# Expert halves split earlier in the last batch, and the first plan cut into pieces between the queries

## The reference

```python
def xattn(query, kv):                     # 16 heads of 32
    q, k = feature_map(query @ Wq.T), feature_map(k_part(kv @ Wkv.T))      # x>0: x+1, else exp(x)
    gate = sigmoid(query @ Wg.T + bg)
    z    = 1 / (einsum(q, k.sum(-2)) + 1e-6)
    return (einsum(q, einsum(k, v)) * z * gate) @ Wo.T
def ffn(x):
    w, sel = top_k(x @ Wr, 2);  w = softmax(w)
    return sum_e gate_e * (x @ We[e] + be[e])
x = x + xattn(layernorm(x), ctx)
x = x + ffn(layernorm(x))
```

## Time and profile before

| | us |
|---|---|
| median of 3 runs | 618.32 (618.17 to 620.92) |
| span of the profiled execution, from its first to its last instruction | 623.2 |
| busy in it: PE, DVE, ACT, POOL | 565.5, 343.8, 198.4, 152.9 |

### The profile page before, as it was taken

The page is one execution under the profiler, slowest core; times in us unless marked ns, Lnnn a source line. Parts: engine busy times, 40 slices in busy tenths (PEclk is TensorE's granted clock), DMA queues, the critical chain, the costliest instruction groups (busy, mean ns, idle before and its releaser), DMA issues.

```text
span 623.2 us, 10341 instructions
## 1 busy us (share of the span) xinstructions
PE 565.5 (91%) x2944; PEld 473.5 (76%) x2945; DVE 343.8 (55%) x889; ACT 198.4 (32%) x348; POOL 152.9 (25%) x179
## 2 busy tenths in 40 slices
PE   6999999999999999999999995998679999988750
PEld 4888888888888788888888884887557788766540
DVE  4453276374347456327636449677886544437753
ACT  5555333534442533532443432234001111111100
POOL 3014201014000003200101436029993000054513
PEclk9999999999999999999999998899779999999985
DMA  9713101313100412200131203457557568679956
GB/s 293 265 35 110 60 1 52 121 67 134 36 0 0 168 34 101 101 0 0 57 121 58 101 25 128 153 167 244 192 161 250 168 197 278 212 257 286 402 206 184
DMA packets 39610, 84.50 MB, mean 136 GB/s; under 512 B 4640, under 2 KB 4640, under 8 KB 39584
## 3 DMA queue, kind: packets, MB, share of 16 engines
q1 hardware_dynamic: 23232, 42.75, 21.5%
q0 software_dynamic: 7424, 25.17, 11.9%
q10 hardware_dynamic: 8928, 16.26, 6.9%
HBM read 52.18 MB, written 31.98 MB: 135 GB/s over the span
## 4 chain that ended last, share of the span: by engine, by line
PE 81%; issue 6%; POOL 6%; DVE 3%; DMA 2%; DVEq 1%; ACT 1%; another core or an unknown queue 1%; POOLq 0%; SPq 0%; ACTq 0%
PE pj L1035 22%; PE pj L1037 21%; PE pj L1036 21%; PE tp L1027 5%; PE kvb L1089 5%; POOL R L490 3%; PE pj L1117 3%; PE tp L1097 2%; PE pj L1043 2%; POOL R L488 1%; DMA num<-y,gidx 1%; DVEq L948 1%; POOL wraw L481 1%; ACT L612 1%; DMA wraw<-in_L_xattn_Wkv_dram 1%
## 5 line engine op out<-in xcount | busy, mean ns | idle before, releaser
L1035 PE MATMUL pj<-R 128*128 128x512 f32 x448 | 185.0, 413 | 3.2 <-DVE R L741 3.2
L1037 PE MATMUL pj<-R 128*128 128x512 f32 x448 | 177.4, 396 | 0.0
L1036 PE MATMUL pj<-R 128*128 128x512 f32 x448 | 176.5, 394 | 0.0
L1035 PEld LDWEIGHTS pj<-R 128*128 128x128 f32 x448 | 85.4, 191 | 19.5 <-DVE R L741 4.4
L1037 PEld LDWEIGHTS pj<-R 128*128 128x128 f32 x448 | 85.0, 190 | 19.2
L1036 PEld LDWEIGHTS pj<-R 128*128 128x128 f32 x448 | 85.6, 191 | 15.6
L1035 PE MATMUL pj<-R,aux 128*128 x184 | 78.2, 425 | 20.9 <-issue 17.6
L1037 PE MATMUL pj<-R,aux 128*128 x184 | 73.9, 402 | 0.0
L1036 PE MATMUL pj<-R,aux 128*128 x184 | 73.7, 400 | 0.0
L651 ACT CAST aux<-tp 128x512 fp32r<-128x512 f32 x46 | 26.9, 585 | 114.2 <-PE tp L1097 84.5
L475 POOL TENSOR_TENSOR rstd<-rstd,mhalf 128x1 f32<-128x1 f32 (+1 forms) x20 | 13.2, 662 | 203.0 <-DVE rstd L759 203.0
(11 more groups left out here) (156 smaller groups left out, 743.0 us busy)
## 6 DMA issues: line engine op xcount, KB each, us to landing
khat<-xs SPq DMA_DIRECT2D x46, 256.0 KB
wraw<-in_L_ffn_We_dram POOLq DMA_DIRECT2D x16, 512.0 KB, 3.9
buf<-in_ctx_dram SPq DMA_DIRECT2D x15, 512.0 KB, 3.8
y<-kvbd ACTq DMA_DIRECT2D x23, 256.0 KB
y<-zeros ACTq DMA_DIRECT2D x23, 256.0 KB
wraw<-in_x_dram SPq DMA_DIRECT2D x4, 1024.0 KB, 7.7
x_rows<-gate SPq DMA_DIRECT2D x3, 1024.0 KB, 5.2
out_dram<-wraw ACTq DMA_DIRECT2D x12, 256.0 KB
```

The source lines that it names most:

```text
L1035: nc.tensor.matmul(bank[:, :], s_hi(k), m_hi(k), start=(k == 0), stop=False)
L1036: nc.tensor.matmul(bank[:, :], s_hi(k), m_lo(k), start=False, stop=False)
L1037: last = nc.tensor.matmul(bank[:, :], s_lo(k), m_hi(k), start=False, stop=(k == KT - 1))
```

## The change

The slots of R are dealt out anew: the first four weights stay where they were, the turned tokens take slots 10 and 11 and the output weight 12 and 13. So the slots of experts 3, 4 and 5 hold only the query weight, the gate weight and the turned tokens, none of which is read after the last gate product. GpSimd now splits the first half of expert 3 once the last batch's last q product is done, and lays the other halves of 3, 4 and 5 between and behind the four scales; only experts 6 and 7 wait for the output products. On VectorE the first plan is advanced by one piece behind each of the last batch's qhat instructions, and the four `index` instructions come behind the queries.

```diff
--- before.py
+++ after.py
@@ -66,13 +66,15 @@
         R = sb("R", [P, 2 * E, KT, D], F32R)
         WK, WV, WQ, WG, WO = range(5)
 
+        W_AT = [2, 4, 6, 8, 12]
+
         def w_hi(n):
-            return R[:, 2 + 2 * n, :, :]
+            return R[:, W_AT[n], :, :]
 
         def w_lo(n):
-            return R[:, 3 + 2 * n, :, :]
-
-        xT_hi, xT_lo = R[:, 12, :, :], R[:, 13, :, :]
+            return R[:, W_AT[n] + 1, :, :]
+
+        xT_hi, xT_lo = R[:, 10, :, :], R[:, 11, :, :]
         ctxT_hi = R[:, 14, 0:2, :].rearrange("p s (k c) -> p s k c", k=KT)
         ctxT_lo = R[:, 14, 2:4, :].rearrange("p s (k c) -> p s k c", k=KT)
         agT_hi = R[:, 15, 0:2, :].rearrange("p s (k c) -> p s k c", k=KT)
@@ -516,11 +518,21 @@
             pool.wait_ge(SEMS["v"], nth("v", last, ST - 1))
             for h in range(4):
                 cut_expert(1 + h // 2, h % 2)
-            for t in range(TT):
-                scale(1, t, 1, "_x2", last, t)
+            pool.wait_ge(SEMS["q"], nth("q", last, G - 1))
+            cut_expert(3, 0)
+            scale(1, 0, 1, "_x2", last, 0)
+            cut_expert(3, 1)
+            scale(1, 1, 1, "_x2", last, 1)
+            pool.wait_ge(SEMS["g"], nth("g", last, TT - 1))
+            cut_expert(4, 0)
+            scale(1, 2, 1, "_x2", last, 2)
+            cut_expert(4, 1)
+            scale(1, 3, 1, "_x2", last, 3)
+            cut_expert(5, 0)
+            cut_expert(5, 1)
             pool.wait_ge(SEMS["wo"], nth("wo", last, TT - 1))
             nc.gpsimd.memset(bias[:, :], 0.0).then_inc(zeroed, 1)
-            for e in range(3, E):
+            for e in range(6, E):
                 for h in range(2):
                     cut_expert(e, h)
             for t in range(TT):
@@ -849,7 +861,7 @@
                 link(nc.vector.bn_aggr(mv[:, 1, t, :], stats[:, :]))
                 centre(1, t, 1, "mean_x2")
 
-            def queries(b):
+            def queries(b, planning=()):
                 for step, kind, i in QUERIES:
                     if step == "T" and kind == "c":
                         if b is LAST:
@@ -862,6 +874,7 @@
                         dve.wait_ge(SEMS["expq"], nth("expq", b, i))
                         nc.vector.scalar_tensor_tensor(qhat[:, i, :], expq[:, i % 2, :], 1.0, qhat[:, i, :],
                                                        ALU.min, ALU.add).then_inc(SEMS["qhat"], 1)
+                        next(planning, None) if b is LAST else None
                     elif step == "G":
                         if i == 0:
                             dve.wait_ge(x2_stored, b * 16 + 16)
@@ -937,11 +950,9 @@
                 keys(b + 1, b)
                 assert n_step[0] == start + per, (n_step, start, per)
             n_step[:] = [start + per * (B - 1), 0, 0]
-            for _ in plan(0, vones.rearrange("p s g c -> p (s g c)")):
-                pass
+            queries(B - 1, plan(0, vones.rearrange("p s g c -> p (s g c)")))
             for c in range(4):
                 index(c, c)
-            queries(B - 1)
 
             def copy_y(m, slot, n):
```

## The result

The changed kernel takes 618.08 us (median of 20 runs, 616.25 to 619.89) against 619.85 us for the kernel before in 20 runs (617.49 to 622.73): a ratio of 0.9967, 95% interval 0.9956 to 0.9978. By the ratio that is 2.0 us less, where 0.6 us more was forecast. It is small, but the interval leaves no doubt of its sign. The forecast time, 618.9 us, lies only 0.8 us from 618.08, but that is luck: it was built on 618.32 us for the kernel before, which takes 619.85 us over these 20 runs.

The account below looks back on a forecast made before the run. TensorE bounds the kernel, idling where GpSimd's splits hold VectorE, at the last batch's queries and in START. Terms 5.0 + 1.0 + 1.5 - 6.9 = +0.6 us on the 618.32 median gave 618.9 us, range 611.5 to 625.

Parts of the forecast that it names:

- Term 1: At the last batch's queries, held plan pieces on VectorE delay qhat 3 and so attention product A0: +5.0 us.
- Rival (d): VectorE instructions arriving while GpSimd only issues a load run at once; A0 2.1 us less, 616.8 us; chance 0.08.
- Terms 2 and 3: Expert 3's second half holds L853 of token tile 3, +1.0 us; scales queued behind halves delay expert tile 2, +1.5.
- Rival (c): BN_STATS and moments behind residual 2 are held too; START begins 3 to 5 us later, 622 to 624 us; chance 0.20.
- Term 4: In START, splitting ends earlier; a lag of 7.5 us at tile 2 becomes 0.6 at tile 10: -6.9 us.
- Rival (b): START regains more, up to 9.4 us by tile 10, giving 615.4 us; chance alone 0.08.

Follow-up runs that it names:

- e3: Kernel before, with GpSimd splitting experts 1 and 2 only when the first plan is finished; 614.39 us against 619.82, ratio 0.9910.
- e8: Changed kernel without the splits of experts 5, 6 and 7 and their loads; 606.51 us against 619.64, ratio 0.9761.
- e2: Kernel before with only the plan cut into pieces between the queries; 620.6 us against 619.82, ratio 1.0007.
- e4: Changed kernel with the whole plan ahead of the queries and GpSimd waiting for it before experts 1 and 2; 608.65 us, ratio 0.9814.
- e5: Changed kernel, pieces kept, with GpSimd waiting for the finished first plan before splitting experts 1 and 2; 613.64 us against 619.64, ratio 0.9896.
- e6: Changed kernel with expert 4's two halves behind the four scales instead of between them; 619.43 us against 619.64, ratio 0.9988.
- e10: e4 with the fourth scale ahead of expert 4's second half instead of behind it; 609.17 us against 618.95, ratio 0.9837.
- e1: Changed kernel with the first plan and gidx instructions run whole ahead of the last batch's queries; 617.6 us against 619.82, ratio 0.9974.
- e7: e4 with GpSimd waiting for the fourth qhat instead of the plan before experts 1 and 2; 613.21 us against 619.64, ratio 0.9887.

## Why the prediction was wrong

**What bounds the kernel** was read rightly: VectorE is held by GpSimd's splits in both places (e3, e8).

**Term 1 (+5.0; measured +3.3 at A0)** is the term that was mis-sized most, and the step that failed is "Piece 1 has four held instructions ... let through at 377.5, 380.0, 382.1 and 384.5". Only two of the four were held. L906 was let through behind the CAST, and L909 ran right behind it (376.61, 0.25 us), before the TENSOR_TENSOR took over; L913 was let through behind that TENSOR_TENSOR, and L915, which I had down for a grant of its own, started 0.36 us behind its end (379.51 against 379.15) and ran in 0.16 us. Qhat 1 at 379.89 was the next to be held, to the end of the CAST at 381.21, and was done at 381.77, where 385.5 was forecast, 384.65 on this execution's clock, whose mark lies 0.85 us earlier. I had allowed one instruction of VectorE for each of GpSimd's; here a second one passed twice, L909 0.14 us before the TENSOR_TENSOR at 376.75 and L915 0.36 us behind the end of one. It does not always: L913 of the kernel before came right behind L912, which had been let through, and was held. In piece 2 the count of holds by the new half was right, two, but they fell on L922 and L925 instead of L919 and L920, so that less of the piece was left behind the last of them; that it ended at 388.75 and not at 388.25 gave half a microsecond back. The mechanism was right, and e2 prices the new half at 2.6 us of the 3.3.

**Rival (d)**, that an instruction passes while GpSimd only issues a load, did not happen: L906 stood from 375.01 to 376.69 although the CAST that GpSimd took up came at 375.61, and qhat 1 stood from 379.89 although its CAST came at 380.16. They came 0.47 and 0.74 us behind the end of a TENSOR_TENSOR; L915, 0.36 us behind one, was not held. The load starts 0.30 us behind a TENSOR_TENSOR's end; L915 came 0.07 us into it, the other two 0.17 and 0.45. One row shows the load holding VectorE by itself: L793 at 436.34, 0.17 us when alone (455.76), took 0.40 and ended at 436.74, when the load from 436.05 to 436.77 ended; no CAST followed it, only the memset. Its counterparts in e4, e5, e6 and e10 took 0.40 to 0.48 at the same place. So (d) was wrong about the load. The Trainium skill ("SBUF — State Buffer", "Who interferes with whom") has the instruction that issues first keep the ports for its whole length. The holds of VectorE to a GpSimd instruction's end agree with it; these two do not by the times of the CASTs, unless the issue of a load takes the ports as well; and the time that I had worked out for it, 2.1 us less, came close to the measured A0 for another reason.

**Terms 2 and 3 (+2.5 together; measured 5.1 at tile 2 less 3.3 at A0, 1.8).** L853 was held as foretold, 1.95 us instead of 0.69, of which 0.4 us arrived at tile 0 (51.92 behind the mark, 48.22 before: 3.7 late). The other 1.4 came by tile 2, which waits for the scales (e6). Rival (c) did not come: the moments behind the residuals stayed at their own lengths, and the four gidx instructions, held for 1.22 us instead of 0.38 at 422.29, delayed nothing, since the low half behind them waited for ScalarE.

**Term 4 (-6.9; measured -7.6,** from a lag of 5.1 at tile 2 to -2.5 at the second plan). Splitting ended 84.6 us behind the mark, where the forecast has 87.6 (457.0 less 369.45): START began 2.4 us earlier than forecast, and the splits with it. The pace behind it was right: tile 10 starts 17.2 us behind tile 5 (471.04), with 17.0 forecast. What released tile 5 was not. It starts 0.64 us behind the last split (453.87), as I had said, but by coincidence: its low half was ready at 451.70, and TensorE had been at work without a gap since tile 4 at 448.29. The last instruction that the splits kept back for TensorE was tile 4's low half, 4.9 us before they ended, not K0. And 1.4 of the 7.6 us are not shown to be the splits' at all: they are the kernel before's wait ahead of tile 10, 8.9 us behind its last split, and e2, whose splitting ends at the same distance from the mark within 0.3 us, has no such wait. Rival (b), a regain of 9.4 us, did not come in full.

The sum was +0.6, the marks have -2.5 and the times -2.0. Term 1 came out 1.7 us lower than taken, terms 2 and 3 together 0.7, term 4 another 0.7: three small misses on one side, which changed the sign of a difference between 7.5 us lost and 6.9 regained.

What stays open: the time between the second plan and the end. There TensorE waits three times for a tile's load in the changed kernel, 1.7 us in all, and never in the kernel before; no run isolates this. The marks at the second plan and the ratios (times 620 us) agree within 2.3 us: e1 wins 3.3 us at the mark and 1.6 by its ratio, e2 1.0 and nothing, e8 12.6 and 14.8, the others within some 1 us. The marks of each kernel are those of one execution, and the kernel before's wait ahead of tile 10 is in all these differences.

## What to carry to other kernels

Where GpSimd works through large SBUF instructions, a short two-operand instruction of VectorE can cost up to the rest of one of them (2.11 us for one column), so it pays to keep short dependent chains and bulk GpSimd work apart in time. A single wait that let a 5.5 us chain run alone was worth 5 us by itself (e3) and 9 us with the splits brought forward (e4 against e1), while the pieces, which move the chain into the gaps between the queries, gained nothing that can be told (e1, e2). Silence that lasted 6 us longer gave about half of it back (e5, e7), and an earlier beginning of START gave nothing (e6, e10): in this stretch what counts is when the splitting ends.

## What the runs showed of the hardware

- VectorE's four qhat instructions (128x512, both operands in SBUF) took 2.7 us in the kernel before, where GpSimd was idle, and 8.41 beside the splits (e3).
- The hold works both ways: GpSimd's TENSOR_TENSOR of 2.39 us took 2.68 and 2.61 us where a VectorE instruction had been let through just ahead of it (381.30 and 386.14 in the changed kernel).
- Behind a GpSimd instruction more than one VectorE instruction can pass, but it is a close race: L906 and L909, L913 and L915 passed in the changed kernel. In e1 a CAST of VectorE (L926) at 381.58 took 0.18 us beside a TENSOR_TENSOR that starts at 381.57, and the TENSOR_SCALAR 0.09 us later was held for 2.34; the same CAST in the kernel before, at 382.18 with the TENSOR_TENSOR, was held for 2.39.
- GpSimd's issuing of a load holds VectorE as well: L793 took 0.40 us at 436.34 beside the load of 436.05 to 436.77, and 0.17 us at 455.76. It is not every instruction: its counterpart in e2, at 437.69 between a TENSOR_TENSOR and a CAST, took 0.17.
- The instructions with one operand in SBUF and one in PSUM were not held in the changed kernel's START: expert tile 5's low half (L757) took 0.69 us in the changed kernel at 451.01, beside GpSimd's TENSOR_TENSOR from 450.83 to 453.23.
